# Cross-attention and expert layers on one core: in some periods VectorE reads two banks of maxima one by one, and the next writer waits for the first bank alone

## The reference

```python
kv_input = jnp.concatenate([x, lat], axis=1)     # 6404 context rows + 1024 tokens = 7428 keys
q = lat @ Wq                                      # 16 heads of 64 values
k, v = jnp.split(kv_input @ Wkv, 2, axis=-1)
dots = jnp.einsum('bhid,bhjd->bhij', q, k) * scale
attn = jax.nn.softmax(dots, axis=-1)              # needs each token's maximum over 7428 keys
out = jnp.einsum('bhij,bhjd->bhid', attn, v)      # then out @ Wout
```

## Time and profile before

| | |
|---|---|
| three runs | 2420.95, 2423.75, 2425.65 us; median 2423.75 |
| profiled execution | span 2422.2 us from first to last instruction; no time of its own beside the span is recorded |
| busy share of the span | PE 94%, PEld 61%, DVE 76%, ACT 69%, POOL 77% |
| attention stage (`stage_attention`, heads) | about 123 to 2066 us |
| mean granted TensorE clock | 0.978 of full speed over the span |

### The profile page before, as it was taken

How to read it: one execution, slowest core, us unless ns; L and a number is a source line. 1 busy time by engine, 2 the same in 40 slices (tenths; PEclk the granted TensorE clock), 3 DMA queues, 4 the chain that set the end, 5 groups by cost and what they waited for, 6 DMA issues and landing times. The chain is left out here.

```text
span 2422.2 us, 68504 instructions
## 1 busy us (share of the span) xinstructions
PE 2278.6 (94%) x27967; PEld 1476.3 (61%) x27967; DVE 1851.0 (76%) x2815; ACT 1674.6 (69%) x3028; POOL 1860.4 (77%) x1124
## 2 busy tenths in 40 slices
PE   2899999999999999999999999999999999779996
PEld 1356665566556655666566656665666665557885
DVE  8878888888788878888888788878888772348775
ACT  4677777777777777777777777777777777246663
POOL 1788899889988898889888988898889999340001
PEclk8899999999999999999999999999999999789998
DMA  2431314132413141314131413142313000240000
GB/s 89 120 81 42 95 62 121 41 92 66 117 43 95 59 119 44 93 51 122 51 92 44 124 61 92 41 115 67 92 42 106 25 2 2 87 125 1 2 2 12
DMA packets 124634, 165.68 MB, mean 68 GB/s; under 512 B 26392, under 2 KB 100192, under 8 KB 123872
## 3 DMA queue, kind: packets, MB, share of 16 engines
q1 hardware_dynamic: 122176, 157.53, 23.2%
q10 hardware_dynamic: 2144, 3.77, 0.5%
HBM read 99.28 MB, written 61.97 MB: 67 GB/s over the span
## 5 line engine op out<-in xcount | busy, mean ns | idle before, releaser
L631 POOL TENSOR_TENSOR att_prob_low<-att_prob 128x1024 f16<-128x1024 f32 x960 | 1767.0, 1867 | 191.3 <-PE all_banks L751 151.6
L908 ACT ACTIVATE att_prob<-all_banks 128x512 f32<-128x512 f32 x1888 | 1070.7, 591 | 386.2 <-PE all_banks L716 263.1
L1002 DVE TENSOR_REDUCE att_part<-all_banks 128x2 f32<-128x1024 f32 x800 | 946.7, 1218 | 195.3 <-PE all_banks L676 195.3
L737 PE MATMUL all_banks<-att_v,att_prob 128*128 128x129 f16 x5664 | 583.6, 220 | 2.9 <-DVE shared_att L1026 0.6
L737 PEld LDWEIGHTS all_banks<-att_v,att_prob 128*128 128x128 bf16 x5664 | 414.2, 98 | 237.9 <-issue 10.3
L751 PEld LDWEIGHTS all_banks<-att_v,att_prob_low 128*128 128x128 f16 x7552 | 328.6, 98 | 135.4 <-POOL att_prob_low L631 15.9
L697 PE MATMUL all_banks<-att_qc,att_kc 128*128 128x512 f16 x1056 | 401.2, 380 | 0.0
L698 PE MATMUL all_banks<-att_qd,att_kd 128*128 128x512 f16 x1056 | 401.0, 380 | 0.0
L751 PE MATMUL all_banks<-att_v,att_prob_low 128*128 128x65 f16 x7552 | 385.1, 194 | 11.4 <-POOL att_prob_low L631 11.3
L741 PE MATMUL all_banks<-att_v,att_prob 128*128 128x64 f16 x1888 | 371.1, 197 | 0.0
L739 PE MATMUL all_banks<-att_v,att_prob 128*128 128x65 f16 x1888 | 365.7, 194 | 0.0
(11 more groups left out here) (313 smaller groups left out, 3042.1 us busy)
## 6 DMA issues: line engine op xcount, KB each, us to landing
v_all<-att_stage_v SPq DMA_DIRECT2D x98, 258.0 KB, 2.7
att_kc<-k_high SPq DMA_DIRECT2D x90, 232.0 KB, 3.9
att_v<-v_all SPq DMA_DIRECT2D x28, 483.8 KB
att_v<-v_all SPq DMA_DIRECT2D x28, 451.5 KB
k_high<-att_stage_h SPq DMA_DIRECT2D x98, 128.0 KB, 1.7
k_low<-att_stage_l SPq DMA_DIRECT2D x98, 128.0 KB, 1.9
att_kd<-k_low SPq DMA_DIRECT2D x45, 232.0 KB, 4.3
att_kc<-k_high SPq DMA_DIRECT2D x30, 232.5 KB, 4.4
```

The costliest lines, as they stand in the source:

```text
L631: pool.tensor_tensor(prob_low[g % NL][:, 0:w], p[:, 0:w], p.bitcast(BF16)[:, 1:2 * w:2], op=ALU.subtract).then_inc(low_split, 1)
L737: pe.matmul(O[:, q, :], w, v[:, e, t, :], start=first, stop=False, skip_group_check=True)
L908: act.activation(prob[g % NP][:, i * BANK:(i + 1) * BANK], S[n % 3], ACT.Exp, scale=SCALE)\
L1002: dve.tensor_reduce(parts[:, n:n + 2], pers.banks[:, 4 + 2 * pair:6 + 2 * pair, :], axis=AX.X, op=ALU.max)\
```

## The change

`take` gets a flag. In the periods whose bank 4 is used by side work, pair 0 is read bank by bank, by two instructions over 512 values in place of one over 1024; and `side` waits until one more bank is read, not two, before PE writes bank 4. Nothing else is changed.

```diff
+        def side_bank_used(b, e, w, projecting):
+
+            return projecting and task_at(e, w) is not None or w in (BACK_AT, FRONT_AT)
...
                 if n is not None:
-                    pe.wait_ge(max_taken, 2 + m * SLOTS + WINDOW * k + 2)
+                    pe.wait_ge(max_taken, 2 + m * SLOTS + WINDOW * k + 1)
                     project(i + 1, n, Y)
                 elif w == BACK_AT or (w == FRONT_AT and with_max):
                     if with_max:
-                        pe.wait_ge(max_taken, 2 + m * SLOTS + WINDOW * k + 2)
+                        pe.wait_ge(max_taken, 2 + m * SLOTS + WINDOW * k + 1)
                     spread_top(b if w == BACK_AT else b + 1, 1 if w == BACK_AT else 0)
...
-            def take(m, k, pair):
+            def take(m, k, pair, one_by_one=False):
 
                 n = WINDOW * k + 2 * pair
                 dve.wait_ge(max_scored, m * SLOTS + n + 2)
-                if (n + 1) % K_CHUNKS and (n + 2) % K_CHUNKS:
+                if (n + 1) % K_CHUNKS and (n + 2) % K_CHUNKS and not one_by_one:
...
-                        take(m, k, 0)
+                        take(m, k, 0, side_bank_used(b, e, w, projecting))
                         take(m, k, 1)
```

## The result

The kernel takes 2392.82 us (median of 4 runs, 2392.12 to 2394.76), beside 2422.35 us before (4 runs, 2418.67 to 2425.65). The ratio is 0.988, with a 95% interval of 0.986 to 0.989: 29.5 us less, where the sum said 28.5. The profiled execution took 2392.94 us, its span is 2390.8. From span to span it is 31.4 us less (2422.2 to 2390.8), 2.9 more than the sum; the closer match of the medians is partly chance.

A forecast was written before the change was run, and what follows sets the result against it. PE was taken as the bound, starting side work late while DVE reads a bank pair. Gains of 21.2 + 5.2 + 2.1 = 28.5 us gave a 2393.7 us span, 2395.2 us median; range 2390 to 2404 (forecast's own 2391 to 2400).

The forecast's parts named there:

- the sum: Total predicted gain over the kernel: 21.2 + 5.2 + 2.1 = 28.5 us.
- The loop within a period: PE writes four banks, DVE reads the first pair in 1.22 us, PE's other work is 0.15 us shorter.
- rival 2: PE's starts are not the bound; only waits booked by the wait view return, 6 us: 2418 us, chance 0.04.
- rival 4: DVE's first single read frees its bank only with the second, 0.07 us later than now: 2437 us, chance 0.01.
- 21.2 us from 141 projections: Late projections outside period 14 each get back 0.15 us at the wait ahead of side work.
- 5.2 from period 14: The 14 projections in period 14 of heads 0 to 13 each get back 0.37 us.
- 2.1 from period 13: The spreads in period 13 of heads 0 to 13 get back 14 x 0.15 us.
- Period 27 at nothing: The spread there counted as no gain: the stretch goes by ACT, which does not get its bank sooner.
- Head 14 at nothing: Its two spreads counted as no gain, since POOL works there 48.20 us without a pause.
- The added reads: 219 more DVE instructions, 0.07 us each, 15 us in all, costed at nothing: covered by DVE's wait for ACT's copy.
- Rival 3: DVE becomes waited for through subtraction and seed, deciding once 0.15 + x exceeds 0.47 us: 2427 us, chance 0.01.
- Rival 1: Part of the gain is given back to another wait close behind; if half goes, about 2409.5 us, chance 0.12.

The follow-up runs named there:

- x1_reads_only: Changed kernel, reads still bank by bank, but PE waits for both banks as in the kernel before: 2421.86 us, ratio 0.998.
- x2_period14: Changed kernel with the bank-by-bank read and shorter wait in period 14 alone, other periods as before: 2417.96 us, ratio 0.997.
- x3: Changed kernel, but DVE reads bank 4 alone and banks 5 to 7 by one instruction: 2390.52 us, ratio 0.985.
- x5_pad384: Changed kernel plus one unused DVE read of 384 values ahead of the second pair in each period with a projection: 2392.76 us, ratio 0.987.
- x9_pad640: Changed kernel plus one unused DVE read of 640 values ahead of the second pair in each period with a projection: 2429.23 us, ratio 1.001.
- x10: x8 with the spread's second copy made by DVE instead of ACT, as in x7_nm_on_dve: 2372.80 us, ratio 0.977.
- x11_no_relu: Changed kernel with the edits of x3 and x6_late_add alone, ReLU quarters left on DVE: 2367.32 us, ratio 0.974.
- x6_late_add: Changed kernel with the normalization's last addition (of the rests) called 14 periods later, in periods 28 and 13: 2378.42 us, ratio 0.979.
- x7_nm_on_dve: Changed kernel with the second copy of the spread maxima in periods 13 and 27 on DVE instead of ACT: 2389.16 us, ratio 0.985.
- x8: Changed kernel with the edits of x3 and x6_late_add, and the ReLU's last two quarters of the first expert layer on ACT: 2368.95 us, ratio 0.977.

## Why the prediction was right

- **The loop within a period, read from the starts of matmuls.** Right. The wait view booked 3.2 us of waits at L654; the change gave 29.5, so rival 2 (only booked waits come back) falls, and all 254 gaps closed, so rival 4 (the bank is not released sooner) falls too. `x1_reads_only` has the reads and not the wait and gains nothing: the wait is the cause.
- **21.2 us from 141 projections, 5.2 from period 14, 2.1 from period 13.** 0.155, 0.369 and 0.157 us each, where 0.15, 0.37 and 0.15 were put: 21.9 + 5.2 + 2.2 = 29.3. `x2_period14` shows the second alone. Of the stage's 31.2 us another 1.2 are period 27's (below), some 1.1 are three single delays of 0.35 us that the profiles of before and of `x2_period14` have and no other, and the last 0.4 is mostly head 0's first period, 0.34 us shorter; over all profiles that one varies from 3.2 to 4.7 us. Head 15, without projections, takes 0.8 back. That isn't the change's doing either: head 15 lasts 110.9 us before and in `x3`, 111.8 in `x1`. So the three terms measure 29.3 us; apart from period 27 the rest of the 31.4 us from span to span is what varies from run to run.
- **Period 27 at nothing.** Mis-sized. It gives 0.09 to 0.10 us in each head, of which odd heads lose 0.04 in period 29 to POOL. The step that was wrong is "ACT does not get its bank sooner". I took ACT's copy for one that follows the exponentials without delay, since it starts 0.03 us before their drawn end. But where ACT has all it needs it starts sooner than that: after the change the copy starts 0.11 us before the drawn end, 0.97 us after the start of the two exponentials and no longer 1.06. So before the change the copy was held up for 0.09 us by PE's spread, under a drawn end, just as PE was. Only the other 0.06 of 0.15 us is lost to ACT, and the start of L713 behind L710 grew by as much, from 0.14 us to 0.21. After the change, head 2, ACT's exponentials and copy and the two matmuls:

```profile
471.79 1.08 ACT L912 ACTIVATE att_prob<-all_banks 128x512 f32<-128x512 f32 x2 [0.54 <-PE all_banks L720]
472.76 0.59 ACT L902 ACTIVATE att_qd<-all_banks 64x512 f16<-64x512 f32 x1
...
474.85 0.38 PE L710 MATMUL all_banks<-att_qc,att_kd 64*128 64x512 f16 x1
475.06 0.39 PE L713 MATMUL all_banks<-att_qd,att_kd 64*128 64x512 f16 x1
```

- **Head 14 at nothing.** Period 13 gives 0.16 and 27 gives 0.10 us, and periods 14 and 29 take 0.14 and 0.07 back: 0.06 us is left, where the sum has nothing.
- **The added reads, 0.07 us each and covered.** Right in price (1.21 against 1.14 us start to start). The cover was 0.32 us and not 0.25, since the single read also starts 0.07 us sooner, which I did not have. Counted from start to start it is 0.41 us (`x5_pad384`). The price of 125 ns (the Trainium skill, Perfetto Trace Analysis, Optimizing Scalar/DVE Operations) is above what this overlapped case shows; as the prediction said, the sum did not hang on it.
- **Rival 3's threshold.** Its mechanism is real (`x9_pad640`), its point was put too low: an added 0.32 us in all should have decided. With the split read's 0.07, 0.53 us still cost nothing and 0.80 did.
- **Rival 1.** No wait behind took a share in the periods with projections; only the end of a half did, by 0.04 us in odd heads.

## What to carry to other kernels

Where a wait is shorter than a matmul is drawn, neither the idle column nor the wait view shows it: compare start with start, and a period that waits with one that doesn't. The same holds for ACT, as period 27 shows. When a reader has idle time behind it, let it release first what the waiter needs first, alone, and take the rest in one piece (`x3`): that costs no instruction. Count a cover from start to start, and when two edits stand in the same list, ask what the first does to the start of the second (`x10`).

## What the runs showed of the hardware

**A single-bank read starts sooner.** DVE's idle behind the same window of PE is 0.55 us ahead of a one-bank read of 512 values (`after`, `x1`, `x3`) and 0.62 ahead of a two-bank read (before), though both wait for the same scores.

**DVE can be held by POOL for much longer than one instruction of it.** Between tiles in SBUF, DVE's work has very unequal durations. The addition of two SBUF tiles takes 0.36 us when POOL is idle (second row); in `x11_no_relu` it takes 5.54 and 5.28 us in head 14 and twice 9.18 in head 15, where POOL works through 27 units of 1.85 us without a pause. DVE's and POOL's timelines in head 15:

```profile
1950.86 9.18 DVE L1038 TENSOR_TENSOR shared_att<-shared_att,att_rest 128x192 f32<-128x192 f32 x1
...
2019.03 0.36 DVE L1038 TENSOR_TENSOR shared_att<-shared_att,att_rest 128x192 f32<-128x192 f32 x1
```

```profile
1909.79 50.03 POOL L635 TENSOR_TENSOR att_prob_low<-att_prob 128x1024 f16<-128x1024 f32 x27 [1.03 <-ACT att_prob L912]
1959.99 1.04 POOL L635 TENSOR_TENSOR att_prob_low<-att_prob 128x512 f16<-128x512 f32 x1 [0.17 <-POOL att_prob_low L635]
```

The addition ends at 1960.04, 0.22 us after POOL's chain pauses at 1959.82: it lasted over the ends of five of POOL's units, up to the first pause. The other three long ones also end 0.21 to 0.22 us after the start of a pause of 0.17 us in POOL's chain. The Trainium skill (SBUF — State Buffer, Who interferes with whom) says that DVE and GpSimd share a port pair as an exclusive lock, that an operation with two SBUF inputs contends with GpSimd's reads, and that the first to issue blocks the other for an instruction. The traces agree that an operation of this kind is held up while POOL works, but not that it is for one instruction: here it lasts over several. The ReLU of 17.5 us in `x6_late_add` and one of 17.0 us in `x7_nm_on_dve` (0.69 is its least) also stand beside back-to-back work of POOL; but the ReLU has one SBUF input, not two, and that the cause is the same is not shown. Of 51 runs of the kernel before 13 were 12 to 20 us above the median of the others. Over all kernels with the quarters on DVE it was some 27 of 124 (10 to 22 us above the others of their kernel); of the 12 runs with the quarters on ACT (`x8`, `x10`) none was, but of the 6 of `x11`, which leaves them on DVE, none was either. So the ReLU as the cause of those runs is seen in two profiles and not settled by the timed runs. Nor is it settled why in `x10`, as in some periods of `x11` (2.07 us), the addition got through at the end of one of POOL's units without a pause.
